# A graph layer and a routed feed-forward layer on one core: own rows copied out tile by tile, x loaded in parts of 2, 4 and 4 tiles, expert tiles as straight code

## What is computed

```python
# layer 1: relational graph layer, x already layer-normed
xs = x[src]                                              # 20000 edges, sorted by dst
total = sum_r (xs @ W_rel[r] + b_rel[r]) * where(edge_type == r, edge_weight, 0)     # 4 relations
agg = segment_sum(total, dst) / max(segment_sum(edge_weight, dst), 1)
x1  = layer_norm(x + x @ W_self + b_self + agg)
out = layer_norm(x1 + gelu(x1 @ W_ffn1 + b1) @ W_ffn2 + b2)                          # 512 -> 1024 -> 512
# layer 2: 16 experts, top 2 of a softmax router, each 512 -> 256 -> 512 with gelu
out = sum_e gate[:, e] * (gelu(xt @ w1[e].T + b1[e]) @ w2[e].T + b2[e])
```

## Time and profile before

| | |
|---|---|
| median of 3 runs | 677.15 us (675.43 to 677.49) |
| the profiled execution's own time | 674.45 us |
| its span | 672.5 us |
| TensorE matmuls busy | 529.1 us, 79% of the span |
| VectorE / ScalarE / GpSimd busy | 318.8 / 118.5 / 231.2 us |
| mean granted clock of TensorE | 0.887 of full speed |
| DMA | 125.47 MB, 187 GB/s over the span |

### The profile page before, as it was taken

How to read it: one execution, slowest core, us unless ns; L and a number is a source line. 1 busy time by engine, 2 the same in 40 slices (tenths; PEclk the granted TensorE clock), 3 DMA queues, 4 the chain that set the end, 5 groups by cost and what they waited for, 6 DMA issues and landing times.

```text
span 672.5 us, 7258 instructions
## 1 busy us (share of the span) xinstructions
PE 529.1 (79%) x2292; PEld 356.9 (53%) x2293; DVE 318.8 (47%) x845; ACT 118.5 (18%) x250; POOL 231.2 (34%) x269
## 2 busy tenths in 40 slices
PE   1799999999960199999999999934728889989500
PEld 1588888887610165565665757522226656666300
DVE  5596573212300714598695999567401122222144
ACT  0501001000110032232322222112003222222000
POOL 2740000037676057777677200000730011110173
PEclk9999999969976589999999999965558999999955
DMA  8454242247699047777676288070542487783286
GB/s 286 180 167 162 95 156 94 94 128 210 195 401 393 1 121 209 202 195 203 175 203 196 78 321 335 1 314 2 208 182 91 132 310 249 246 284 112 70 247 214
DMA packets 47538, 125.47 MB, mean 187 GB/s; under 512 B 6336, under 2 KB 6976, under 8 KB 45200
## 3 DMA queue, kind: packets, MB, share of 16 engines
q0 software_dynamic: 17344, 63.20, 30.3%
q1 hardware_dynamic: 26912, 54.95, 21.8%
q10 hardware_dynamic: 3248, 6.89, 3.4%
HBM read 85.70 MB, written 39.32 MB: 186 GB/s over the span
## 4 chain that ended last, share of the span: by engine, by line
PE 69%; issue 9%; POOL 7%; DVE 6%; DMA 6%; ACT 2%; ACTq 1%; POOLq 0%; SPq 0%; DVEq 0%
PE ps L814 11%; PE ps L825 9%; PE ps L947 7%; PE ps L754 7%; PE ps L755 7%; PE ps L756 7%; PE ps L964 7%; PE ps L780 5%; POOL greg L563 3%; POOL xslot L537 3%; PE ps L940 2%; POOL greg L516 2%; DMA w_in<-w_rel 2%; PE ps L791 2%; DMA greg<-xslot 1%
## 5 line engine op out<-in xcount | busy, mean ns | idle before, releaser
L516 POOL DMA_INDIRECT greg<-msg,row_i x157 | 155.3, 989 | 178.5 <-DMA msg<-greg 101.5
L754 PE MATMUL ps<-w_hi,xT_hi 128*128 128x512 f32 x200 | 80.7, 403 | 1.7 <-DVE xT_lo L1041 1.7
L755 PE MATMUL ps<-w_lo,xT_hi 128*128 128x512 f32 x200 | 80.0, 400 | 0.0
L756 PE MATMUL ps<-w_hi,xT_lo 128*128 128x512 f32 x200 | 80.0, 400 | 0.0
L814 PE MATMUL ps<-freg,wreg 128*128 128x256 f32 x320 | 71.5, 382 | 0.8 <-ACT freg L613 0.8
L825 PE MATMUL ps<-wreg,freg 128*128 128x512 f32 x160 | 72.1, 598 | 0.0
L814 PEld LDWEIGHTS ps<-freg,wreg 128*128 128x128 f32 x320 | 60.1, 190 | 16.3 <-issue 7.5
L947 PE MATMUL ps<-wreg,freg 128*128 x224 | 55.3, 391 | 0.0
L964 PE MATMUL ps<-wreg,freg 128*128 x112 | 52.8, 593 | 0.9 <-ACT freg L700 0.9
L780 PE MATMUL ps<-greg,sel 128*32 128x512 f32 x320 | 46.2, 636 | 5.8 <-DMA greg<-msg,row_i 5.8
L537 POOL DMA_INDIRECT xslot<-work,pos_i x20 | 19.7, 986 | 85.5 <-DVE pos_i L1318 79.8
(11 more groups left out here) (170 smaller groups left out, 645.7 us busy)
## 6 DMA issues: line engine op xcount, KB each, us to landing
wreg<-experts POOLq DMA_DIRECT2D x11, 1025.0 KB, 6.2
msg<-greg SPq DMA_DIRECT2D x40, 256.0 KB, 2.0
xslot<-greg SPq DMA_DIRECT2D x1, 8960.0 KB, 25.5
greg<-xslot SPq DMA_DIRECT2D x28, 256.0 KB, 3.7
yslot<-greg SPq DMA_DIRECT2D x28, 256.0 KB, 2.4
wreg<-experts SPq DMA_DIRECT2D x5, 1025.0 KB, 9.7
wreg<-w SPq DMA_DIRECT2D x8, 512.0 KB, 12.8
w_in<-w_rel ACTq DMA_DIRECT2D x3, 1024.0 KB, 6.1
```

The costliest lines, as they stand in the source:

```text
L516: nc.gpsimd.indirect_dma_start(gath[:, c % RING, :], None, msg, bass.IndirectOffsetOnAxis(ap=row_i[:, c:c + 1], axis=0)).then_inc(s_gath[c ...
L754: nc.tensor.matmul(bank(t % 5), xT_hi[:, at], w_hi[:, i, wk], start=(k == 0), stop=False)
L755: nc.tensor.matmul(bank(t % 5), xT_hi[:, at], w_lo[:, i, wk], start=False, stop=False)
L756: mm = nc.tensor.matmul(bank(t % 5), xT_lo[:, at], w_hi[:, i, wk], start=False, stop=(k == KD - 1))
```

## The change

SP issues x in parts of 2, 4 and 4 tiles with relation 0's weights after the first part, and takes over the two loads of the vectors. ScalarE does one small copy first, splits relation 0's weights in two halves ahead of the tiles, and issues the load of relation 1's weights after tile 2. The low part of relation 0's weights is split between VectorE and GpSimd. TensorE transposes three tiles, then does a product of relation 0 and the transpose of a later tile in turn; VectorE's low parts of x are woven into its statistics, norms and evacuations. Relations 1 to 3 are written out. `work` is saved in ten transfers, each after its tile's evacuation in the self product. The expert loop is written out on ScalarE and TensorE.

```diff
@@ -33 +33 @@
 PAIRS = NT // 2
+HEADS = ((0, 2), (2, 6), (6, NT))
 RSQRT_SEED = 0x5f3759df - (3 << 23) - (1 << 31)
@@ -277 +278 @@
-        s_xh = [sem(f"x_half_in{h}") for h in range(2)]
+        s_xh = [sem(f"x_tiles_in{h}") for h in range(len(HEADS))]
         s_edge = sem("edges_in")
...
         s_cst = sem("constants")
+        s_warm = sem("scalar_tables_in")
         s_fill = sem("constants_cleared")
@@ -391 +393 @@
         def _(sp):
-            for h in range(2):
-                a, b = h * NT // 2, (h + 1) * NT // 2
+            for h, (a, b) in enumerate(HEADS):
                 sp.dma_start(x_res[:, a:b, :], x[a * P:b * P, :].rearrange("(t p) d -> p t d", p=P)).then_inc(s_xh[h], 16)
-            load_product_weights(sp, 0)
+                if h == 0:
+                    load_product_weights(sp, 0)
             for a, b in ((dst_i, dst), (src_i, src), (typ_i, typ), (w_e[:, :], wgt)):
...
             sp.dma_start(base_i, dst[0:1, :].rearrange("a n -> (a n)").partition_broadcast(P)).then_inc(s_edge, 16)
+            sp.dma_start(bias, vecs[0:V_G1, :].rearrange("v d -> (v d)").partition_broadcast(P)
+                         .rearrange("p (v d) -> p v d", v=V_G1)).then_inc(s_vec, 16)
+            sp.dma_start(vec[:, :, :], vecs[V_G1:NV, :].rearrange("v d -> (v d)").partition_broadcast(P)
+                         .rearrange("p (v d) -> p v d", v=NV - V_G1)).then_inc(s_vec, 16)
             with sp.Fori(0, REL) as r:
...
+            for t in range(NT):
+                sp.wait_ge(s_evac, FREE + NT * REL + t + 1)
+                sp.dma_start(own_rows[t * P:(t + 1) * P, :], work[:, t, :]).then_inc(s_own, 16)
             sp.wait_ge(s_prod, NT * (REL + 1))
...
                              w2[k * P:(k + 2) * P, :].rearrange("(k p) n -> p k n", p=P)).then_inc(s_ffw, 16)
-            sp.wait_ge(s_evac, FREE + NT * (REL + 1))
-            sp.dma_start(own_rows.rearrange("(t p) d -> p t d", p=P), work[:, :, :]).then_inc(s_own, 16)
             sp.wait_ge(s_zeros, 1)
@@ -489 +495 @@
             pool.wait_ge(s_cst, 2)
-            for h in range(2):
-                half = slice(h * NT // 2, (h + 1) * NT // 2)
+            for h, (a, b) in enumerate(HEADS):
                 pool.wait_ge(s_var, h + 1)
-                nc.gpsimd.tensor_tensor(rs[:, half], var[:, half], mhalf[:, half], ALU.pow).then_inc(s_rs, 1)
-            pool.wait_ge(s_whi, 1)
-            nc.gpsimd.tensor_tensor(w_lo[:, 0, :], w_in[:, :], w_hi[:, 0, :], ALU.subtract).then_inc(s_wlo, 1)
+                nc.gpsimd.tensor_tensor(rs[:, a:b], var[:, a:b], mhalf[:, a:b], ALU.pow).then_inc(s_rs, 1)
+                if h == 0:
+                    pool.wait_ge(s_whi, 2)
+                    nc.gpsimd.tensor_tensor(w_lo[:, 0, KD * D // 2:], w_in[:, KD * D // 2:], w_hi[:, 0, KD * D // 2:],
+                                            ALU.subtract).then_inc(s_wlo, 1)
@@ -567 +573 @@
         def _(act):
+            act.wait_ge(s_cst, 2)
+            nc.scalar.copy(sm[:, 12:13], mhalf[:, 0:1]).then_inc(s_warm, 1)
             act.wait_ge(s_win, 16)
-            act.dma_start(bias, vecs[0:V_G1, :].rearrange("v d -> (v d)").partition_broadcast(P)
-                          .rearrange("p (v d) -> p v d", v=V_G1)).then_inc(s_vec, 16)
-            act.dma_start(vec[:, :, :], vecs[V_G1:NV, :].rearrange("v d -> (v d)").partition_broadcast(P)
-                          .rearrange("p (v d) -> p v d", v=NV - V_G1)).then_inc(s_vec, 16)
+            for h in range(2):
+                half = slice(h * KD * D // 2, (h + 1) * KD * D // 2)
+                nc.scalar.copy(w_hi[:, 0, half], w_in[:, half]).then_inc(s_whi, 1)
+            for t in range(NT):
+                act.wait_ge(s_xnT, t + 1)
+                nc.scalar.copy(xT_hi[:, t * D:(t + 1) * D], bank(5 + t % 3)).then_inc(s_xhi, 1)
+                if t == 2:
+                    act.wait_ge(s_wlo, 2)
+                    load_product_weights(act, 1)
             act.dma_start(bf1_s[:, :], bf1).then_inc(s_ffw, 16)
...
-            for t in range(NT):
-                if t == 3:
-                    act.wait_ge(s_win, 16)
-                    nc.scalar.copy(w_hi[:, 0, :], w_in[:, :]).then_inc(s_whi, 1)
-                act.wait_ge(s_xnT, t + 1)
-                nc.scalar.copy(xT_hi[:, t * D:(t + 1) * D], bank(5 + t % 3)).then_inc(s_xhi, 1)
             for i in range(1, REL + 1):
-                act.wait_ge(s_wlo, i)
-                load_product_weights(act, i)
+                if i > 1:
+                    act.wait_ge(s_wlo, i + 1)
+                    load_product_weights(act, i)
                 act.wait_ge(s_win, 16 * (i + 1))
@@ -725 +734 @@
             expert_tiles(0)
-            with act.Fori(1, LOOPED) as it:
+            for it in range(1, LOOPED):
                 expert_tiles(it)
@@ -737 +746 @@
-            for t in range(NT):
+            def turn_xn(t):
                 pe.wait_ge(s_xn, t + 1)
-                if t >= 3:
-                    pe.wait_ge(s_xlo, t - 2)
+                after(pe, s_xlo, t - 2)
                 for k in range(KD):
@@ -756 +764 @@
-            pe.wait_ge(s_xlo, NT)
-            with pe.Fori(0, REL // 2) as r2:
-                for i in range(2):
-                    pe.wait_ge(s_wlo, r2 * 2 + (i + 1))
-                    for t in range(NT):
-                        product(i, t, r2 * (2 * NT) + (i * NT + t))
+            for t in range(3):
+                turn_xn(t)
+            pe.wait_ge(s_wlo, 2)
+            for t in range(NT):
+                pe.wait_ge(s_xlo, t + 1)
+                product(0, t, t)
+                if t + 3 < NT:
+                    turn_xn(t + 3)
+            for r in range(1, REL):
+                pe.wait_ge(s_wlo, r + 2)
+                for t in range(NT):
+                    product(r % 2, t, r * NT + t)
@@ -847 +861 @@
-            pe.wait_ge(s_wlo, REL + 1)
+            pe.wait_ge(s_wlo, REL + 2)
             for t in range(NT):
@@ -1000 +1014 @@
             expert_tiles(0)
-            with pe.Fori(1, LOOPED) as it:
+            for it in range(1, LOOPED):
                 expert_tiles(it)
@@ -1017 +1031 @@
-            for h in range(2):
+            def x_stats(h):
+                a, b = HEADS[h]
                 dve.wait_ge(s_xh[h], 16)
-                tiles = range(h * NT // 2, (h + 1) * NT // 2)
-                for t in tiles:
+                for t in range(a, b):
                     own.did(v.bn_stats(st[:, t, :], x_res[:, t, :]))
                 sync(own)
-                for t in tiles:
+                for t in range(a, b):
                     own.did(v.bn_aggr(mv[:, t, :], st[:, t, :]))
                 sync(own)
-                half = slice(tiles.start, tiles.stop)
-                v.tensor_scalar(var[:, half], mv[:, half, 1], EPS, None, ALU.add).then_inc(s_var, 1)
-            for t in range(NT):
-                dve.wait_ge(s_rs, 1 if t < NT // 2 else 2)
-                v.tensor_scalar(work[:, t, :], x_res[:, t, :], mv[:, t, 0:1], rs[:, t:t + 1],
-                                ALU.subtract, ALU.mult).then_inc(s_xn, 1)
-            dve.wait_ge(s_xn, NT)
-            for t in range(NT):
+                v.tensor_scalar(var[:, a:b], mv[:, a:b, 1], EPS, None, ALU.add).then_inc(s_var, 1)
+            def x_norm(h):
+                dve.wait_ge(s_rs, h + 1)
+                for t in range(*HEADS[h]):
+                    v.tensor_scalar(work[:, t, :], x_res[:, t, :], mv[:, t, 0:1], rs[:, t:t + 1],
+                                    ALU.subtract, ALU.mult).then_inc(s_xn, 1)
+            def x_low(t):
                 dve.wait_ge(s_xhi, t + 1)
...
+            x_stats(0)
+            x_norm(0)
+            dve.wait_ge(s_whi, 1)
+            v.tensor_tensor(w_lo[:, 0, 0:KD * D // 2], w_in[:, 0:KD * D // 2], w_hi[:, 0, 0:KD * D // 2],
+                            ALU.subtract).then_inc(s_wlo, 1)
+            x_stats(1)
+            x_low(0)
+            x_low(1)
+            x_norm(1)
+            x_stats(2)
+            x_low(2)
+            x_low(3)
+            x_norm(2)
+            x_low(4)
@@ -1088 +1115 @@
-                dve.wait_ge(s_whi, nth)
+                dve.wait_ge(s_whi, nth + 1)
                 v.tensor_tensor(w_lo[:, i, :], w_in[:, :], w_hi[:, i, :], ALU.subtract).then_inc(s_wlo, 1)
...
                 r, t = n // NT, n % NT
-                if t == 0:
+                if t == (5 if r == 0 else 0):
                     low_part((r + 1) % 2, r + 2)
+                if n < NT - 5:
+                    x_low(n + 5)
                 dve.wait_ge(s_prod, n + 1)
@@ -1209 +1238 @@
                 if s == 3:
-                    dve.wait_ge(s_own, 16)
+                    dve.wait_ge(s_own, 16 * NT)
                     fast_first_norm(0)
...
             for p in range(PAIRS):

```

## The result

The changed kernel takes 640.75 us in the median of 4 runs (639.41 to 640.88), against 676.29 for the kernel before in the median of 4 beside it: ratio 0.9472, 95% interval 0.9445 to 0.9499. The profiled execution took 639.41 us. Now and then an execution of a kernel takes 10 us or more longer than its others; the ratios leave such executions out, the medians do not, and the profile of f0_changed_again (685.7 us against 672.9 to 675.9) stands in no table for that reason.

The account below looks back on a forecast made before the run. TensorE was taken to work nearly without a break, so time is won only in its chain's holes, the largest 22.80 us. Gains 21.4 + 5.8 + 2.0 = 29.2 take 677.15 to 647.9 us, range 643 to 654.

Parts of the forecast that it names:

- Own rows: At TensorE's 22.80 us hole: saving own_rows tile by tile ahead of the FFN weight loads lets the norm start earlier, gain 21.4.
- Rival 1: Before the transpose of x1: late FFN weights stop TensorE instead, the hole shrinks by only 17.4, about 652 us; chance 0.07.
- Rival 4: At the 22.80 us hole: gathers or weights released VectorE, the hole stays, only 7.8 gained, about 669 us; chance 0.04.
- The start: From kernel start through relation 0: earlier first product, transposes woven between products, relation 0 ends at 49.0 instead of 54.8, gain 5.8.
- forecast 16.1: At the start: TensorE's first product begins at 16.1 us instead of 26.77.
- Transposing a tile costs 0.61: In relation 0: seven tiles transposed between products, taken at 0.7 us each with the change of operands, 4.9 together.
- Rival 2: At the start: VectorE's low parts or x come late, gain 2 instead of 5.8, about 652 us; chance 0.14.
- Experts: At the expert tiles: straight code shortens four TensorE gaps from 8.39 to 6.4 us, gain 2.0, bounds 0 and 3.4.
- I take 1.6 each: At the expert tiles: each of four TensorE gaps takes 1.6 us as straight code, 6.4 together.
- the 1.3 to 1.9: Sign at the expert tiles: TensorE's gaps there would measure 1.3 to 1.9 us once written out.
- the first jump alone: At the expert loop: by the fetch rule alone only the first jump back paid a fetch, making the gain 1.1.
- Rival 3: At the unrolled products and tiles: straight code waits for instruction fetches of 1.1 us, about 681 us at 30; chance 0.03.

Follow-up runs that it names:

- f0_changed_again: The changed kernel, nothing altered, run once more on kind B: 675.55 us against 701.77 for the kernel before, ratio 0.96.
- k1: The kernel before with only the ten tile-by-tile saves of own rows, on kind A: 653.74 us against 675.16, ratio 0.9673.
- h2: The changed kernel, nothing altered, run again on kind A: 641.25 us against 674.95 for the kernel before, ratio 0.9495.
- h3: The changed kernel with each expert group's register table loads moved behind the previous group's last second product, on kind A: 633.74 us, ratio 0.9411 to the kernel before.
- kind A: The runs in which the kernel before takes 675 to 677 us; whether the chip or its condition makes the kind is not known.
- e6: The changed kernel with its ten saves put behind the FFN weight loads on SP's queue, on kind B: 686.17 us, ratio 0.979 to the kernel before.
- f1: The changed kernel with one single save ahead of the FFN weight loads instead of ten, on kind B: 673.26 us, ratio 0.9601 to the kernel before.
- k2: The changed kernel with one save and the expert loops kept, so the new start alone, on kind A: 666.52 us against 675.16, ratio 0.988.
- h1: The kernel before, nothing altered, traced again in one execution on kind A: 674.0 us.
- kind B: The runs in which the kernel before takes 701 to 702 us; whether the chip or its condition makes the kind is not known.
- f2: The changed kernel with the pair sums' 40 small matmuls spread four behind each product of relation 3, on kind B: 682.79 us, ratio 0.9717 to the kernel before.

## Why the prediction was wrong, point by point

**Own rows: right in cause and size.** Forecast 21.4; G fell by 21.4 between the two profiles (to 57 in k1, h2 and h3, 2 us more), and own rows alone gave 21.4 in the medians (k1). That both agree to the tenth is in part luck: in the means of the profiles of kind A, G is 80.3 with the old save and 57.7 with the new one, 22.7. Rival 1 (late weights) is out: they made TensorE wait 0.76 to 2.4 us in the profiles of kind A with the new save, each time ahead of a longer wait for VectorE. Rival 4 (the save isn't the cause) is out by e6. That the saves were split, which the prediction costed in detail, didn't matter (f1).

**The start: mechanism right, the term mis-sized.** Forecast 5.8, measured 7.2 between the profiles and 8.6 for the start alone (k2; its ratio's interval times 675 is 4.7 to 11.5). The first product came at 15.56, forecast 16.1: 0.5. The step that failed is "Transposing a tile costs 0.61 ...; I take 0.7 with the change of operands": it cost 0.44, and seven of them 3.1 instead of 4.9, 1.8 in all. The 0.61 was taken from tiles ahead of the first product, the wrong neighbourhood: after the change the four transposes at 14.79 take 1.12 and those between products 0.60, of which the next product covers a part. Against it stands 0.9 that the first matmuls lose by their wider spacing. In the first profile of the kernel before, that loss happened not to occur (P 112.3); with the old start P was 112.3 three times and 113.6 to 113.9 five times, and just in these five the granted clock is at 0.50 for some 3.4 us around the first products. So most executions of the kernel before lose 1.5 there, and h1 against h2 (first pair sum at 141.2 and at 132.4, 8.7) shows more than the profile that the forecast was built on. Rival 2 (the start gives little) is out.

**Experts: the term mis-sized.** "I take 1.6 each": the four gaps took 1.50, 1.52, 0.88 and 1.16, 1.27 in the mean, two of them below the 1.3 to 1.9 that the prediction named as its sign. Gain 3.3, and 0.3 more behind the group, against 2.0 with an upper bound of 3.4. The one row for a straight passage, 1.85, was the first execution of its kind and the worst guide; the later ones are shorter in every profile. Nor is it the first jump alone that had paid: over all profiles the gaps with the loop are 2.20 to 2.25, 2.52 to 3.17, 1.66 to 1.74, 1.65 to 1.73 and 0.68 to 0.72, and straight 1.50 or 1.51, 1.50 to 1.59, 0.87 to 1.07, 0.86 to 1.16 and 0.34 to 0.42. The Trainium skill (Runtime: NRT & Kernel Launch, "Instruction fetch mechanics") has a taken branch stall when its target is outside a small window of fetched code. By the prediction's reading of it only the first jump back would pay; that gap did shrink the most (by 1.3 of 3.7), but the trace doesn't agree that the others pay nothing, since they shrank by 0.3 to 0.8 each. What a turn of the loop costs isn't taken apart either: written out, the code loses its jumps, and its table addresses and wait values become constants instead of sums in registers, and no run separates the two. Rival 3 (straight code costs) is out.

**A term that was missing: the clock between the pair sums and the window sums.** C was 20.6 in the profile before and 17.4 in the one after: 3.2 us that no part of the change made, since own rows alone has had 17.4, 19.0 and 20.6 of it, and the kernel before 19.0 the second time; the time at the lower clock accounts for it (10.3 and 3.4 us, above). The prediction's row showed the clock at 0.50 in one place only; it didn't ask where else the clock falls and whether it falls alike in each execution, so its range had no room for it.

**The sum.** From 647.9 to 640.75 are 7.2 us: start 1.4, experts 1.4 in E, the clock 3.2, and 1.4 because the median lies 1.3 above the profiled execution after and was taken as 2.7 above before. These are 7.4, less some 0.2 in other stages. With the two terms sized as measured (2.8) the forecast would have been 645.1, inside the range; the other 4.6 come from the single executions on which it was built and by which it is read, and they carry it out.

Not all of that is chance. In the means of the profiles of kind A the start is worth 8.4, own rows 22.7 and straight tiles 3.1, together 34.2, near the 33.7 of h2. So the three terms were 5.0 too small in sum, the start's the most (2.6), and 677.15 less 34.2 is 643.0, the lower bound of the range. The last 2.2 are what differs from execution to execution.

## What to carry to other kernels

A store that guards an overwrite belongs on its queue where its data is ready, ahead of bulk loads that are needed later: its place was worth 21 us here (kind A), and its size nothing (kind B, the only one on which that was tried). Register loads from a table belong behind issued matmuls, not at the head of a group: moving them gave 7.5 us, more than writing out the loop around them (3.4). When a sum is made from one execution, look first for the stretches in which the clock falls, and give the range their spread.

## What the runs showed of the hardware that was not expected

- **The clock behind small matmuls.** Among or just behind 40 matmuls of one column in one run the granted clock fell to 0.50 in every profile, for 3.4, 6.8 or 10.3 us, and C took 17.4, 19.0 or 20.6 us with it, by execution and not by kernel. With four of them between full products it stayed at 1.00 (one profile, f2).
- **The clock behind a gap.** After the gap of 2.5 to 3.2 us at the first jump back, three profiles of the eight with the loop show the next first products (1.9 us at full clock) at 2.9 to 3.6, and a fourth (k1) shows 3.1 behind the gap of 2.20 at the entry. Of the eight with straight code none does behind the gap of 1.5 to 1.6 in its place. The profile of k2, for one:

```profile
543.86 1.09 PE L953 MATMUL ps<-ident,greg 128*128 128x128 f32 x4 [2.93 <-issue]
544.74 3.62 PE L960 MATMUL ps<-wreg,freg 128*128 x8
548.15 2.71 PE L977 MATMUL ps<-wreg,freg 128*128 x4
```

- **Two kinds of runs.** Every kernel's pairs took 181 to 182 us on kind A and 203 to 206 on kind B, and G without the hole 57 to 59 and 64 to 67. On B TensorE waits more, at a lower clock (own rows alone, windows of 250 to 400 us: busy 149.20 of 150 at 1.00 on A, 137.48 at 0.94 on B, DMA 211 and 155 GB/s). The waits there are put down to "issue", so the cause isn't shown. With the hole G is 80 to 83 on both kinds, so the hole covers some 7 us of this, and closing it gives about 15 in G on B and 23 on A. Own rows alone measured 16 to 19 and 21.
